# Self-attention and cross-attention of a decoder layer on one core: the batch loops written out, and VectorE's work in self-attention in another order

## The chip, the core and the metric

The kernel runs on one core of a Trainium2 chip. A core has five engines that run side by side, each from its own queue and in its order: TensorE (PE in the profile; its weight loads are listed apart as PEld), VectorE (DVE), ScalarE (ACT), GpSimd (POOL) and SyncE (SP), which here only issues transfers. They wait for each other by semaphores. The metric is the time of one execution in microseconds (us) on the device; lower is better.

## The reference

The layer takes x (16 batches, 100 tokens, 512 features) and a context (16 batches, 722 keys, 512 features). In short:

```python
x = x + attn(layernorm(x))            # 64 heads of 32 in four branches, rotary positions, sinks
x = x + xattn(layernorm(x), ctx)      # 16 heads of 32, softmax over the 32 largest of 722 scores
x = x + ffn(layernorm(x))             # a product with a 512x512 matrix in the frequency domain
```

```python
# attn, per batch (B, H, T, DH)
q = rope(rms_norm(X @ WQ + bQ));  k = rope(X @ WK + bK);  v = X @ WV + bV
w = (q @ k.T) / |k| * branch_mask
probs = softmax([w, tanh(sink)])
out = probs[..., :T] @ v + probs[..., T:] * v_nulls
y = mean over the four branches of (out @ WO + bO)
```

What the change touches is in `attn`: rms_norm and rope of the projected q and k, and the softmax's denominator.

## The kernel before

The program has three parts, one after the other. `self_program` computes the first line of the reference for all batches and writes x1 to DRAM. `spectral_program` (not touched) builds the 512x512 matrix M of the last line. `cross_program` computes the second and third line.

**Self-attention.** One batch's q of three branches and its k are 2048 columns, four segments of 512. The function `body(b, ...)` of each engine is written as a software pipeline: a body does the attention of batch b (`cur`), the output of batch b-1 (`prev`), the projections of batch b+1 (`nxt`) and the layer norm of batch b+2 (`far`). `each_batch` writes out bodies -2 to 1 and 14 to 16 and puts a hardware loop (`eng.Fori`) around one body for batches 2 to 13. Inside the loop the wait counts are computed in registers from the loop's counter.

TensorE's body, in order: it spreads the reciprocal of the denominators over partitions (L629), turns segment 0 of the rotated q and k (`turn(0)`, four transposes, L616), computes the values of the third branch (`value(2)`, L600), `turn(1)`, transposes the next batch's normalised x (L642), `turn(2)`, `turn(3)`, the output product of the batch before (L651), and then four times a group of four heads' scores and one segment of the next batch's projection (both L88 to L90, each product split in three), two value products (also L88 to L90), the denominators (L708) and the numerators (L716).

VectorE's body: `low(g)` (L506) makes the low half of the turned segment g, after ScalarE has made its high half; `turn(1)` waits for `low(0)` and `turn(3)` for `low(1)`, since they write into the same PSUM bank. Three products by the spread reciprocals (L530) and two sums (L532, L535) give the context, for which the output product waits. `biased(n)` (L511) takes segment n of the projection out of PSUM; `squares(n)` (L517, L520) sums ScalarE's squares of it; GpSimd raises these sums to the power -0.5 (`power(n)`, L362); `rope(n)` (seven instructions, L483 to L491) scales and rotates the segment. `statistics` (L95 to L97) and `normalised` (L501) are the layer norm of batch b+2. The reciprocal of the denominators (L579) waits for L708 of TensorE, and L629 of the next body waits for it. GpSimd also masks the scores of each group of four heads (L351) ahead of `power(1)`.

The second value product on TensorE waits until `biased(3)` has emptied its PSUM bank.

**Cross-attention.** It works on 13 tiles of scores a batch (128 rows of 722 keys), in seven steps of two tiles. VectorE finds the 32 largest of each row by four rounds of MAX8 and MATCH_REPLACE8 (L1368 to L1390), and also does a few layer norm instructions (L1400 is one). ScalarE does the exponentials and copies, GpSimd subtractions and low halves. `each_batch` there loops seven times over two bodies, batches 1 to 14, and writes out the others.

Of the kernel before, what the change touches and what calls it, by code (L numbers as in the profile page):

```python
# [23 lines left out]
B, T, D, KV = 16, 100, 512, 722  # L24
# [155 lines left out]
def self_program(nc, A, x1_dram, y3_dram):  # L180
# [5 lines left out]
    QC = NQK // 128  # L186
# [4 lines left out]
    with ExitStack() as ctx:  # L191
# [90 lines left out]
        def each_batch(eng, body):  # L282


            body(At(-2), cur=False, prev=False, nxt=False, far=True)
            body(At(-1), cur=False, prev=False, nxt=True, far=True)
            body(At(0), cur=True, prev=False, nxt=True, far=True)
            body(At(1), cur=True, prev=True, nxt=True, far=True)
            with eng.Fori(2, B - 2) as i:
                body(At(0, i), cur=True, prev=True, nxt=True, far=True)  # L290
            body(At(B - 2), cur=True, prev=True, nxt=True, far=False)
            body(At(B - 1), cur=True, prev=True, nxt=False, far=False)
            body(At(B), cur=False, prev=True, nxt=False, far=False)
# [151 lines left out]
        def _(dve):  # L445
# [29 lines left out]
            def body(b, cur, prev, nxt, far):  # L475
# [49 lines left out]
                if prev:  # L525

                    dve.wait_ge(num_mm, b.count(HK, 0))
                    for n in range(NL):
                        dve.wait_ge(rb_ready, b.count(NL, n + 1 - NL))
                        dve.tensor_tensor(rb[:, n, :], pq[:, n, 0:CC * T], rb[:, n, :], ALU.mult).then_inc(num_used, 1)  # L530
                    dve.wait_ge(num_used, b.count(NL, 2 - NL))
                    order.mark(dve.tensor_tensor(rb[:, 0, :], rb[:, 0, :], rb[:, 1, :], ALU.add))  # L532
                    dve.wait_ge(num_used, b.count(NL, 0))
                    order.after(order.n)
                    dve.tensor_tensor(rb[:, 0, :], rb[:, 0, :], rb[:, 2, :], ALU.add).then_inc(ctx_ready, 1)  # L535
                if cur:
                    for g in range(1, QC // 4):
                        low(g)
                if nxt:

                    dve.wait_ge(xT_hi, bn.count(1, 1))
# [12 lines left out]
                if nxt:  # L554
                    at = bn.const if bn.reg is None else bn.reg + bn.const
                    dve.tensor_reduce(xsum[:, :, bass.ds(at, 1)], xT[:, :, :], AX.X, ALU.add).then_inc(sum_ready, 1)

                    biased(0)
                    biased(1)
                    squares(0)  # L560
                    biased(2)
                    squares(1)
                    rope(0)
                    biased(3)
                    squares(2)
                    squares(3)
                if far:
                    statistics()
                if cur and not nxt:

                    each = lambda t: t[:, :].unsqueeze(2).broadcast_to((128, CC, B))
# [6 lines left out]
                    dve.wait_ge(den_mm, b.count(HK, HK))  # L578
                    dve.reciprocal(rden[:, :], pq[:, 3, 0:T]).then_inc(rden_ready, 1)  # L579
                if nxt:  # L580
                    rope(1)
                    rope(2)
                if far:
                    normalised()
                if nxt:
                    rope(3)
                order.finish()
            each_batch(dve, body)

# [162 lines left out]
def cross_program(nc, A, M, x1_dram, y3_dram, out_dram):  # L752
# [17 lines left out]
    with ExitStack() as ctx:  # L770
# [91 lines left out]
        def each_batch(eng, body):  # L862

            body(At(-1), 1, tiles=False, prev=False, nxt=True)
            body(At(0), 0, tiles=True, prev=False, nxt=True)
            with eng.Fori(0, (B - 2) // 2) as i:
                body(At(1, i, 2), 1, tiles=True, prev=True, nxt=True)
                body(At(2, i, 2), 0, tiles=True, prev=True, nxt=True)
            body(At(B - 1), 1, tiles=True, prev=True, nxt=False)
            body(At(B), 0, tiles=False, prev=True, nxt=False)  # L870

# [619 lines left out]
```

## Time and profile before

| | |
|---|---|
| three runs | 2444.17, 2447.41, 2450.51 us; median 2447.41 |
| the profiled execution | 2448.53 us, of which its span is 2446.7 |
| self-attention, first to last score group (batch 0 to batch 15) | 78.76 to 716.33 us of the span |
| cross-attention, from VectorE's first steady stretch | about 900 to 2446 us of the span |
| busy over the span | TensorE 87%, VectorE 81%, ScalarE 52%, GpSimd 53% |

The busy shares are means over two parts with different limits: in self-attention VectorE is busy for 64% of the time and TensorE for 90%, in cross-attention VectorE for 98%. So the two are read apart. A bracket in a row of the timeline gives the time that the engine was idle ahead of the instruction and what ended it; "issue" is idle time in which the engine waited for nothing that the profile shows.

### The profile page before, as it was taken

The numbers are of one execution on the slowest core, as the hardware profiler recorded it, in microseconds if no ns is written. First come the engines' busy times: TensorE is split into PE (matmuls) and PEld (weight loads), VectorE is DVE, ScalarE is ACT, GpSimd is POOL, SyncE is SP. The second block draws the span as 40 slices with busy tenths as digits, with TensorE's granted clock in tenths as the row PEclk, the third lists the DMA queues.
The fourth block names the chain that finished last, engine by engine and source line by source line (L and its number), as shares of the span: only waits on it lengthen the run. The fifth ranks groups of instructions, "written<-read, shape, count | busy, mean of one in ns | idle before, by whom it ended". The sixth has DMA issues, their size and how long they took to land. (4 is left out here: it accounts for less than half of the span.)

```text
span 2446.7 us, 54297 instructions
## 1 busy us (share of the span) xinstructions
PE 2122.6 (87%) x19760; PEld 1650.1 (67%) x19760; DVE 1977.5 (81%) x3663; ACT 1265.8 (52%) x2464; POOL 1285.2 (53%) x1473
## 2 busy tenths in 40 slices
PE   2898999989897378999999999999899899899966
PEld 1565555656563267877778778778778788788754
DVE  4666565666642149999999999999999999999995
ACT  3232323223221147666666666676676676676652
POOL 2564554636450336566456565565565565555542
PEclk9999998989888689999999999999999999999987
DMA  5000000000002610010001000100100010001000
GB/s 180 11 15 17 13 17 13 10 19 11 14 15 91 161 28 18 13 36 18 20 25 29 21 24 13 37 18 19 37 18 19 25 29 19 25 13 36 5 5 11
DMA packets 41485, 70.11 MB, mean 29 GB/s; under 512 B 4638, under 2 KB 21166, under 8 KB 41260
## 3 DMA queue, kind: packets, MB, share of 16 engines
q1 hardware_dynamic: 35868, 56.31, 7.6%
q0 software_dynamic: 3632, 7.58, 1.3%
q10 hardware_dynamic: 1760, 3.28, 0.5%
q8 instruction: 134, 2.20, 0.4%
q14 instruction: 91, 0.75, 0.1%
HBM read 60.54 MB, written 9.86 MB: 29 GB/s over the span
## 5 line engine op out<-in xcount | busy, mean ns | idle before, releaser
L1390 DVE MATCH_REPLACE8 ca_W<-ca_top,ca_W 128x722 f32<-128x722 f32 (+1 forms) x624 | 553.0, 892 | 0.0
L1378 DVE MAX8 ca_top<-ca_W 128x8 f32<-128x722 f32 (+1 forms) x624 | 536.7, 897 | 2.2
L997 POOL TENSOR_TENSOR ca_S<-ca_S,ca_W 128x722 f32<-128x722 f32 (+1 forms) x208 | 358.6, 1743 | 276.0 <-ACT ca_W L1253 276.0
L1368 DVE MAX8 ca_top<-ca_S 128x8 f32<-128x722 f32 (+1 forms) x208 | 179.0, 898 | 64.9 <-ACT ca_S L1270 49.3
L1275 ACT ACTIVATE ca_PT<-ca_pT 128x768 f32<-128x768 f32 (+1 forms) x208 | 163.6, 786 | 129.4 <-PE ca_pT L1128 129.4
L974 POOL TENSOR_TENSOR ca_KL<-ca_K,ca_KH 128x384 fp32r<-128x384 f32 (+1 forms) x128 | 122.6, 958 | 183.3 <-ACT ca_KH L1245 180.5
L1253 ACT ACTIVATE ca_W<-ca_W,ca_shift 128x722 f32<-128x722 f32 (+1 forms) x208 | 186.0, 894 | 61.8 <-DVE ca_W L1390 61.4
L1161 PE MATMUL ca_pO<-ca_PT,ca_V 128*32 128x56 f32 (+5 forms) x4608 | 217.0, 225 | 0.0
L88 PE MATMUL ca_pS<-ca_KH,ca_QH 128*128 128x362 f32 (+1 forms) x384 | 150.7, 393 | 70.7 <-ACT ca_S L1270 63.5
L1263 ACT ACTIVATE ca_S<-ca_S,ca_shift 128x722 f32<-128x722 f32 (+1 forms) x208 | 175.8, 891 | 65.3 <-POOL ca_shift L989 65.2
L362 POOL TENSOR_TENSOR sa_ss<-sa_ss,sa_minus_half 100x16 f32<-100x16 f32 x64 | 192.3, 3023 | 22.1 <-DVE sa_ss L520 22.1
L88 PE MATMUL ca_pF<-ca_cH,ca_WkH 128*128 128x338 f32 (+1 forms) x512 | 190.5, 372 | 8.2 <-POOL ca_cL L982 4.7
L1128 PE MATMUL ca_pT<-ca_ident,ca_S 128*128 128x128 f32 (+1 forms) x1248 | 179.1, 280 | 19.3 <-issue 19.3
L1270 ACT ACTIVATE ca_S<-ca_pS 128x722 f32<-128x722 f32 (+1 forms) x208 | 159.3, 766 | 56.8 <-PE ca_pS L90 52.4
L1161 PEld LDWEIGHTS ca_pO<-ca_PT,ca_V 128*32 128x32 f32 x4608 | 186.3, 111 | 0.0
L1387 DVE MATCH_REPLACE8 ca_W<-ca_top,ca_S 128x722 f32<-128x722 f32 (+1 forms) x208 | 184.4, 892 | 0.0
L89 PE MATMUL ca_pF<-ca_cL,ca_WkH 128*128 128x338 f32 (+1 forms) x512 | 176.7, 345 | 0.0
L90 PE MATMUL ca_pF<-ca_cH,ca_WkL 128*128 128x338 f32 (+1 forms) x512 | 175.9, 344 | 0.0
L435 ACT ACTIVATE sa_E<-sa_pq 100x300 f32<-100x300 f32 x256 | 86.2, 426 | 169.5 <-PE sa_pq L90 169.5
L1128 PEld LDWEIGHTS ca_pT<-ca_ident,ca_S 128*128 128x128 f32 (+1 forms) x1248 | 132.8, 142 | 44.4 <-issue 29.7
L344 POOL TENSOR_TENSOR sa_step<-sa_minus_half 1x1 f32<-1x1 f32 x64 | 14.2, 222 | 282.5 <-ACT sa_E L435 282.5
L351 POOL TENSOR_SCALAR_AFFINE_SELECT sa_E<-sa_E 100x400 f32<-100x400 f32 x256 | 150.0, 586 | 17.8
(213 smaller groups left out, 5286.2 us busy)
## 6 DMA issues: line engine op xcount, KB each, us to landing
ca_raw<-in_ctxT SPq DMA_DIRECT2D x32, 384.0 KB, 4.0
ca_raw<-in_ctxT SPq DMA_DIRECT2D x32, 338.0 KB, 3.0
sa_xin<-in_x SPq DMA_DIRECT2D x16, 200.0 KB
sa_xres<-in_x SPq DMA_DIRECT2D x16, 200.0 KB
x_scratch<-sa_x SPq DMA_DIRECT2D x16, 200.0 KB
x_scratch<-y_scratch POOLq DMA_DIRECT2D x16, 200.0 KB, 13.7
ca_xin<-x_scratch SPq DMA_DIRECT2D x16, 200.0 KB
ca_x<-x_scratch SPq DMA_DIRECT2D x16, 200.0 KB
```

The source lines that it names most:

```text
L88: pe.matmul(out, ah, bh, start=start, stop=False)
L89: pe.matmul(out, ah, bl, start=False, stop=False)
L90: return pe.matmul(out, al, bh, start=False, stop=stop)
L362: pool.tensor_tensor(part, part, minus_half[:, 0:NH], ALU.pow).then_inc(norm_ready, 1)
L997: pool.tensor_tensor(S[k][rows, :], S[k][rows, :], W[r][rows, :], ALU.subtract).then_inc(p_ready, 1)
L1128: last = pe.transpose(pT[:, 128 * k:128 * k + t.rows], S[slot(t)][0:t.rows, KEY0[k]:KEY0[k] + 128], ident[0:t.rows, 0:t.rows])
L1161: last = pe.matmul(pO[to:to + DH, NUM + at + q.start:NUM + at + q.stop], V[tp][:, k, 128 * g + to:128 * g + to + DH], PT[:, k, cols], star ...
L1253: act.activation(W[r][rows, :], W[r][rows, :], ACT.Exp, bias=shift[rows, r:r + 1], scale=SCALE).then_inc(f_ready, 1)
L1368: dve.max(top[r][rows, 0:8], S[slot(t)][rows, :]).then_inc(peaked, 1)
L1378: n_of[t.i] = order.mark(dve.max(top[r][rows, 8 * k:8 * k + 8], W[r][rows, :]))
L1387: dve.match_replace(W[r][rows, :], eight, S[slot(t)][rows, :], REMOVED).then_inc(removed, 1)
L1390: ins = dve.match_replace(W[r][rows, :], eight, W[r][rows, :], REMOVED)
```

## The change

1. In `self_program` the loop over batches 2 to 13 is written out: twelve bodies in a row on each engine. In `cross_program` the loop over pairs of batches is written out too: fourteen bodies. No register is needed any more for the wait counts and the addresses of transfers, and no branch is taken.
2. VectorE's body in self-attention has another order. `rope(0)` stands behind `biased(3)`, `squares(2)` and `squares(3)`; `rope(1)` stands behind `statistics`, ahead of the reciprocal; `normalised` stands behind `rope(3)`; and `low(1)` stands ahead of the two sums of the context. No instruction is added or removed, and no other engine's order changes.

```diff
-            with eng.Fori(2, B - 2) as i:
-                body(At(0, i), cur=True, prev=True, nxt=True, far=True)
+            for n in range(2, B - 2):
+                body(At(n), cur=True, prev=True, nxt=True, far=True)
...
                         dve.tensor_tensor(rb[:, n, :], pq[:, n, 0:CC * T], rb[:, n, :], ALU.mult).then_inc(num_used, 1)
+                if cur:
+                    low(1)
+                if prev:
                     dve.wait_ge(num_used, b.count(NL, 2 - NL))
                     order.mark(dve.tensor_tensor(rb[:, 0, :], rb[:, 0, :], rb[:, 1, :], ALU.add))
...
                 if cur:
-                    for g in range(1, QC // 4):
-                        low(g)
+                    low(2)
+                    low(3)
...
                     squares(0)
                     biased(2)
                     squares(1)
-                    rope(0)
                     biased(3)
                     squares(2)
                     squares(3)
+                    rope(0)
                 if far:
                     statistics()
+                if nxt:
+                    rope(1)
...
                     dve.reciprocal(rden[:, :], pq[:, 3, 0:T]).then_inc(rden_ready, 1)
                 if nxt:
-                    rope(1)
                     rope(2)
+                    rope(3)
                 if far:
                     normalised()
-                if nxt:
-                    rope(3)
...
-            with eng.Fori(0, (B - 2) // 2) as i:
-                body(At(1, i, 2), 1, tiles=True, prev=True, nxt=True)
-                body(At(2, i, 2), 0, tiles=True, prev=True, nxt=True)
+            for n in range(1, B - 1):
+                body(At(n), n % 2, tiles=True, prev=True, nxt=True)
```

VectorE in a body of self-attention, from the layer norm's statistics to the first instruction of the second rotated segment. Before:

```order
L95 BN_STATS sa_stats<-sa_xin 100x6
L96 BN_AGGR sa_mv<-sa_stats 100x2
L97 TENSOR_SCALAR sa_mv<-sa_mv 100x1
L579 RECIPROCAL sa_rden<-sa_pq 128x100
L483 TENSOR_TENSOR sa_qk<-sa_qk,sa_ss 100x512
```

The same place now:

```order
L97 TENSOR_SCALAR sa_mv<-sa_mv 100x1
L483 TENSOR_TENSOR sa_qk<-sa_qk,sa_ss 100x512
L484 TENSOR_TENSOR sa_tmp<-sa_qk,sa_sin 100x256
L485 TENSOR_TENSOR sa_rq<-sa_qk,sa_cos 100x16x16
L486 TENSOR_TENSOR sa_tmp<-sa_qk,sa_cos 100x256
L487 TENSOR_TENSOR sa_rq<-sa_qk,sa_sin 100x16x16
L489 TENSOR_TENSOR sa_rq<-sa_rq,sa_tmp 100x16x16
L491 TENSOR_TENSOR sa_rq<-sa_rq,sa_tmp 100x16x16
L584 RECIPROCAL sa_rden<-sa_pq 128x100
```

One whole rotation, seven instructions, stands between the statistics and the reciprocal, where nothing stood. (L584 is the line of the reciprocal in the changed kernel.)

VectorE from the end of one body of self-attention to the start of the next. Before, at the loop's end:

```order
L491 TENSOR_TENSOR sa_rq<-sa_rq,sa_tmp 100x16x16
L82 ISA
L289 REGISTER_ALU
L289 COMPARE_AND_BRANCH
L506 TENSOR_TENSOR sa_qkTl<-sa_pp,sa_qkTh 128x400
L530 TENSOR_TENSOR sa_rb<-sa_pq,sa_rb 128x400 x3
L532 TENSOR_TENSOR sa_rb<-sa_rb 128x400
L535 TENSOR_TENSOR sa_rb<-sa_rb 128x400
```

The same place now:

```order
L82 ISA
L506 TENSOR_TENSOR sa_qkTl<-sa_pp,sa_qkTh 128x400
L530 TENSOR_TENSOR sa_rb<-sa_pq,sa_rb 128x400 x3
L506 TENSOR_TENSOR sa_qkTl<-sa_pp,sa_qkTh 128x400
L535 TENSOR_TENSOR sa_rb<-sa_rb 128x400
L538 TENSOR_TENSOR sa_rb<-sa_rb 128x400
```

The branch is gone, and the second L506 has moved ahead of the two sums (L535 and L538 now).

VectorE between the last tile of an even batch and the first tiles of the next in cross-attention, before:

```order
L1390 MATCH_REPLACE ca_W0<-ca_top0,ca_W0 64x722
L82 ISA
L866 REGISTER_ALU
L866 COMPARE_AND_BRANCH
L1368 MAX ca_top2<-ca_S0 128x8
```

Written out, the two instructions of L866 are not there, on this and on the four other engines.

## Rows read from the trace of the kernel before

**Rows 1.** Windows: length, busy us of each engine (instructions), granted clock, DMA share, GB/s.

```profile
163.70:675.20 511.50, 462.38 (x5329) 297.69 (x5328) 325.41 (x684) 155.16 (x372) 273.31 (x300) 0.92 0.05 14
```

**Rows 2.** Timeline (start, duration, line, [idle before]): first scores, batches 0 and 15.

```profile
78.76 0.60 PE L88 MATMUL sa_pq<-sa_qkTh 32*100 32x300 f32 x4 [1.20 <-DVE sa_qkTl L506]
...
716.33 0.41 PE L88 MATMUL sa_pq<-sa_qkTh 32*100 32x300 f32 x4
```

**Rows 3.** TensorE's waits in 163.7 to 675.2 us: total, times, longest.

```profile
PE sa_pp L616 <- DVE sa_qkTl L506: 44.5, 24, 2.3
PE sa_pp L88 <- DVE sa_qk L511: 4.6, 12, 0.4
```

**Rows 4.** Timeline of TensorE around one loop pass.

```profile
410.44 0.79 PE L616 MATMUL sa_pp<-sa_ident,sa_rq 100*128 100x100 f32 x4 [2.31 <-DVE sa_qkTl L506]
...
414.21 5.18 PE L651 MATMUL sa_pw<-sa_WO,sa_rb 128*100 128x512 f32 x8
419.33 0.41 PE L88 MATMUL sa_pq<-sa_qkTh 32*100 32x300 f32 x4
...
433.27 0.39 PE L90 MATMUL sa_pp<-sa_WqkH,sa_xTl 128*100 128x512 f32 x1
...
441.86 2.24 PE L716 MATMUL sa_pq<-sa_E,sa_V 101*32 101x100 f32 x96
```

**Rows 5.** Timeline of VectorE in the same pass and the start of the next.

```profile
436.09 0.68 DVE L511 TENSOR_TENSOR sa_qk<-sa_pp,sa_bias_qk 100x512 f32<-100x512 f32 x1
...
438.07 0.68 DVE L95 BATCH_NORM_STATS2 sa_stats<-sa_xin 100x6 f32<-100x512 f32 x1
...
439.00 0.15 DVE L97 TENSOR_SCALAR sa_mv<-sa_mv 100x1 f32<-100x1 f32 x1
442.19 0.78 DVE L579 RECIPROCAL sa_rden<-sa_pq 128x100 f32<-128x100 f32 x1 [3.03 <-PE sa_pq L708]
442.89 0.63 DVE L483 TENSOR_TENSOR sa_qk<-sa_qk,sa_ss 100x512 f32<-100x512 f32 x1
...
445.57 0.68 DVE L483 TENSOR_TENSOR sa_qk<-sa_qk,sa_ss 100x512 f32<-100x512 f32 x1
...
448.31 0.54 DVE L501 TENSOR_SCALAR sa_xn<-sa_xin,sa_mv,sa_rstd 100x512 f32<-100x512 f32 x1
...
451.81 0.57 DVE L506 TENSOR_TENSOR sa_qkTl<-sa_pp,sa_qkTh 128x400 fp32r<-128x400 f32 x1 [0.23 <-issue]
...
454.41 0.57 DVE L535 TENSOR_TENSOR sa_rb<-sa_rb 128x400 f32<-128x400 f32 x1
```

**Rows 6.** The first rotation's start, and GpSimd's mask (L351) and powers (L362).

```profile
431.76 0.68 DVE L483 TENSOR_TENSOR sa_qk<-sa_qk,sa_ss 100x512 f32<-100x512 f32 x1
...
434.59 2.58 POOL L351 TENSOR_SCALAR_AFFINE_SELECT sa_E<-sa_E 100x400 f32<-100x400 f32 x4
437.14 9.13 POOL L362 TENSOR_TENSOR sa_ss<-sa_ss,sa_minus_half 100x16 f32<-100x16 f32 x3
```

**Rows 7.** Windows around the wait of rows 4, columns as in rows 1.

```profile
407.10:410.50 3.40, 1.09 (x4) 0.26 (x3) 3.14 (x9) 0.60 (x1) 0.00 (x0) 1.00 0.35 120
410.60:417.30 6.70, 5.74 (x20) 3.54 (x20) 4.78 (x10) 2.01 (x4) 0.00 (x0) 0.50 0.00 0
```

**Rows 8.** VectorE's waits from 907.2 to 2336.5 us; windows of two single batches.

```profile
DVE ca_top L1368 <- issue: 15.1, 6, 3.5
...
998.99:1093.13 94.14, 88.42 (x786) 74.50 (x784) 93.51 (x168) 63.72 (x120) 55.84 (x65) 0.98 0.08 24
...
1190.56:1286.54 95.98, 90.08 (x844) 75.79 (x842) 95.34 (x169) 67.80 (x131) 59.84 (x68) 1.00 0.09 24
```

**Rows 9.** TensorE's instruction queue, 60 to 190 us; a written-out batch; cross-attention's loop ends.

```profile
q8 instruction: 10, 0.16, 0.5%
...
699.99 0.71 PE L716 MATMUL sa_pq<-sa_E,sa_V 101*32 101x100 f32 x19 [0.36 <-issue]
...
PE ca_pT L1128 <- issue: 19.3, 6, 4.3
```

## The prediction

> **What bounds the kernel now.** I read the windows first, since the busy shares of the whole span mix two parts. In self-attention TensorE works 462 of 511.5 us and VectorE 325 [rows 1]; in cross-attention VectorE works 93.5 of the 94.1 us of a batch [rows 8]. The change has to be priced in each by itself.
>
> Self-attention takes 637.6 us from the first scores of batch 0 to those of batch 15, fifteen passes of 42.5 us [rows 2], and the twelve passes of the loop take 511.5 / 12 = 42.6 us [rows 1]. TensorE's waits name what ends last there: 24 waits, two a pass, for L506 of VectorE, 44.5 us or 3.7 us a pass, and one a pass of 0.38 us for `biased(3)`, L511 [rows 3]. The timeline shows the long one: `turn(1)` waits 2.31 us for `low(0)` [rows 4], and `low(0)` is the first thing in VectorE's body, so what holds it is what stands at the end of the body before. There VectorE first sat idle for 3.03 us ahead of the reciprocal, which waits for the denominators, and had three rotations still to do behind it [rows 5]. The idle 3 us and the 2.3 us that TensorE waits 10 us later are the same time, lost once on each engine.
>
> The wait costs twice. In the window of the wait TensorE works 1.09 of 3.4 us, and in the 6.7 us behind it the granted clock is 0.50, that is 1.2 instead of 2.4 GHz [rows 7]. The output product falls into it and takes 5.18 us for eight matmuls [rows 4].
>
> Cross-attention runs at VectorE's pace. Its only named idle time between 907 and 2336 us is 15.1 us of "issue" in 6 places [rows 8]: the six taken branches of the loop over pairs of batches. TensorE shows the same six, 19.3 us [rows 9].
>
> **The order in self-attention.** I follow the new chain from TensorE's last projection matmul of a pass to the next scores. Up to there nothing changes: scores at 419.33, last projection matmul over at 433.66, 14.3 us [rows 4]. Then, by the starts of rows 5:
> - `biased(3)`, `squares(2)`, `squares(3)`: 436.09 to 438.07, 2.0 us. They start at 433.7 now, not at 436.09, because `rope(0)` no longer stands ahead. TensorE's 0.38 us wait goes with it.
> - `rope(0)`: 4.33 us today (431.76 to 436.09, rows 5 and 6), because GpSimd masks beside it; a rotation beside GpSimd's powers takes 2.68 us (442.89 to 445.57). Now it starts at 435.7, when the last mask has some 1.0 to 1.4 us left [rows 6]. I take 3.1, between 2.7 and 4.3, near the first because most of the mask is past.
> - `statistics`: 438.07 to 439.15, 1.1 us.
> - `rope(1)`: 2.7 us. It needs `power(1)`, a third of 9.13 us behind the mask, so at 440.2 today and rather earlier when the mask is less disturbed [rows 6]. VectorE arrives at 433.7 + 2.0 + 3.1 + 1.1 = 439.9. The two meet, at a cost of 0 to 0.3 us.
> - reciprocal 0.7 us (442.19 to 442.89). It starts at 442.6 instead of 442.19, while TensorE, 0.38 us earlier, is done with the numerators at 443.7 [rows 4, 5]. The spread of the reciprocals, which alone waits for it, needs it at 443.4 or so: it is just in time, and each later 0.1 us would be paid.
> - `rope(2)` and `rope(3)`: 2.7 us each, `normalised` 0.5, and no branch ahead of `low(0)` (0.23 us of issue today).
> - `low(0)`, three products and the two sums: 451.81 to 454.98, 3.2 us, and `low(1)` between them, 0.5.
>
> Sum: 2.0 + 3.1 + 1.1 + 2.7 + 0.7 + 5.4 + 0.5 + 3.2 + 0.5 = 19.2 us. So `low(0)` ends some 2 us earlier against TensorE, and the 2.31 us wait shrinks to 0.3. What is late next: `turn(3)` waits for `low(1)` still, about 0.7 us, and the output product, which waited for nothing, now waits 0.6 us for the second sum, because TensorE has caught up. `low(1)` ahead of the sums serves the first and delays the second by 0.5. Then the output product: eight matmuls of 0.43 at the full clock, 3.5 us (half of the 5.18 us were run at the low clock). A pass is 14.3 + 19.2 + 3.5 = 37.0 us, with 0.3 us for the semaphores between, 37.3.
>
> **The clock.** This decides 2.6 us of it: 1.7 in the output product and 0.9 in the transposes around it. Today TensorE works 32% of the window that comes ahead of the low clock [rows 7]. In the new chain the 3.4 us from `value(2)` to the output product hold 1.6 us of waits, so it works about half. I take it that the clock mostly stays up and put 0.5 us a pass on the passes where it does not.
>
> **The loops.** In 190 to 655 us no instruction is loaded at all, the loop's bodies stay resident; ahead of it, in 60 to 190 us, TensorE's queue loads 10 blocks of 16 KB for about three batches [rows 9]. Written out, every batch pays that. The load itself is 0.5% of the DMA engines. The price is where TensorE runs out of instructions in the short matmuls of L708, L716 and L629: the one that the profile names, in a batch written out behind the loop, is 0.36 us [rows 9]. I take 0.4 us a pass; bounds 0, since VectorE's chain may hide it, and 0.7 for two of them.
>
> The Trainium skill (Runtime: NRT & Kernel Launch, "Instruction fetch mechanics") says that a straight stream of instructions is loaded ahead and costs next to nothing, and that only a branch out of the loaded window stalls. By it this term would be 0 and the time 6 us less. The trace bears out the branch (up to 3.5 us of issue at a loop end of cross-attention) but shows a stall in a straight stream too, so I keep the row's price.
>
> A pass is 37.3 + 0.5 + 0.4 = 38.2 us. Against 42.5 that is 4.3, and for fifteen passes 64.5 us, all on the path, since the next scores wait for it.
>
> **Cross-attention.** Removed: 15.1 us of issue, at full price, since VectorE has no other wait there for it to fall into. A second gain is likelier than not. The batch ahead of the loop's first branch takes 94.14 us, one behind a branch that holds none takes 95.98, with 1.8 us more of VectorE's work and the same instruction count [rows 8]: after the stall its instructions meet GpSimd's at other moments. Six batches could give up to 1.8 us each back, or all could settle in the worse phase. Bounds -3 and +11; I take 4. No stall for code is added: these bodies were loaded anew in every pass already. Sum 19 us.
>
> **Total.** From the profiled execution, 2448.5 us (1.1 above the median of the three runs, which I ignore): 2448.5 - 64.5 - 19 = 2365.
>
> **Rivals.**
> 1. The clock still falls in every pass. For it: half of the time idle is not much, and several short waits remain. Then a pass is 37.3 + 2.6 + 0.4 = 40.3 us, the gain 2.2 x 15 = 33, with 19 from cross-attention 2396.
> 2. GpSimd sets the pace: `rope(0)` keeps its 4.33 us beside the mask, 1.2 more, and everything behind it on VectorE comes later, the reciprocal too, at 443.8. That is 18 us for fifteen passes, and TensorE's idle time grows by as much, so the clock falls oftener: 2383 to 2414. Against it: the mask ends at 437.1 today even with the rotation beside it. The Trainium skill (SBUF — State Buffer, "SBUF: two separate sides") makes this stronger: a VectorE instruction with two SBUF inputs and a GpSimd one lock each other out for a whole instruction. Beside the masks the trace agrees; beside the powers, which are two-input instructions of 3 us, it does not (rotations at 2.68 us), so I move no rotation's price for them.
> 3. The move gives nothing, because the 3.03 us of idle time only change place: `power(1)` late, the reciprocal behind it. Left are the loops, 19 us, and 0.3 us a pass for the branch: 2425.
> 4. Slower: the code of TensorE does not come in time. In L708 and L716 it takes 192 matmuls and as many weight loads in 4.3 us, so a block of 256 instructions lasts 2.9 us there. If each of about four blocks a pass cost what a loop end in cross-attention costs, 19.3 / 6 = 3.2 us [rows 9], twelve passes would lose 154 us: 2519. It turns to slower from 83.5 / 48 = 1.7 us a block. The 0.36 us stall of a batch that is written out already speaks against it.
>
> **How the numbers follow.** Forecast 0.58, rival 1 0.17, rival 2 0.12, rival 3 0.09, rival 4 0.04. The range: down to 2343, with no term for code or clock (fifteen passes at 37.3, 78 us) and 11 from the phases in cross-attention (26 us); up to 2400, which takes in rival 1 and the better half of rival 2. Outside lie rivals 3 and 4 and a little more. 0.3% of this time is 7 us, about what a measurement of this kernel can tell from no change; faster holds for all rivals but the last and a remnant: faster 0.95, same 0.01, slower 0.04.
>
> **What would show it.** Right: the first scores of batches 0 and 15 stand 573 us apart (560 to 605); VectorE's idle time ahead of the reciprocal is gone; TensorE's wait for `low(0)` is under 0.6 us; the output product takes 3.5 us and the granted clock of self-attention is over 0.95; no "issue" row on VectorE in cross-attention, and batches of 94 to 95 us. Wrong: an output product still at 5 us (rival 1), a first rotation at 4 us (2), TensorE waiting for the reciprocal ahead of L629 (2, 3), gaps of "issue" over 1 us in L708 to L716 of every batch (4).

## The result and the profile after

The changed kernel takes 2351.4 us (median of four runs, 2346.9 to 2352.0) against 2448.7 us before (four runs, 2444.2 to 2450.5): a ratio of 0.960, 95% interval 0.958 to 0.962. The forecast was 2365, with a range of 2343 to 2400. The profiled execution has a span of 2349.5 us, 97.2 less than the 2446.7 of before. I split that by the places that the prediction had named.

| stretch | before, us | after, us | gain | forecast |
|---|---|---|---|---|
| first scores of batch 0 to those of batch 15 (self-attention, 15 passes) | 637.6 | 565.7 | 71.9 | 64.5 |
| from there to the third tile of cross-attention's batch 0 | 190.9 | 188.9 | 2.0 | 0 |
| third tile of batch 0 to that of batch 15 (cross-attention) | 1429.3 | 1411.6 | 17.7 | 19 |
| from there to the end | 110.2 | 104.5 | 5.7 | 0 |

The first place to look at is the timeline of TensorE at the first scores of batches 0 and 15, the lines that answer to [rows 2]:

```profile
78.83 0.60 PE L88 MATMUL sa_pq<-sa_qkTh 32*100 32x300 f32 x4 [1.20 <-DVE sa_qkTl L506]
...
644.52 0.41 PE L88 MATMUL sa_pq<-sa_qkTh 32*100 32x300 f32 x4
```

They stand 565.7 us apart, 37.7 us a pass. Next, the windows of after (columns as in [rows 1]): most of self-attention, one pass of the usual length, and one of two that are longer.

```profile
163.70:630.00 466.30, 448.91 (x5529) 296.71 (x5531) 318.50 (x706) 158.89 (x383) 280.35 (x317) 0.99 0.06 18
...
231.85:269.05 37.20, 35.64 (x445) 23.61 (x444) 25.72 (x57) 12.89 (x31) 22.12 (x25) 1.00 0.06 18
269.05:307.96 38.91, 37.41 (x445) 24.14 (x444) 25.70 (x57) 12.87 (x31) 22.12 (x25) 0.96 0.06 18
```

TensorE now works 448.9 of 466.3 us, 96%, where it worked 462.4 of 511.5, 90% [rows 1]; the mean granted clock went from 0.92 to 0.99. The two passes have the same instructions and the same work on the other engines. They differ in the clock alone, 1.00 against 0.96, and by 1.7 us.

TensorE's waits between 150 and 620 us (total, times, longest) answer to [rows 3]:

```profile
PE sa_pp L619 <- DVE sa_qkTl L506: 9.7, 20, 0.8
PE sa_pw L654 <- DVE sa_rb L538: 8.0, 13, 0.6
PE sa_pt L632 <- issue: 0.2, 1, 0.2
```

The waits for `low`, 44.5 us in the twelve passes of [rows 3], are 9.7 us in this stretch of some twelve and a half, the 4.6 us for `biased(3)` are gone, and a new wait stands in their place, that of the output product for the second sum. The timeline of TensorE at the end of the usual pass shows where each lies (compare [rows 4]):

```profile
262.40 0.53 PE L619 MATMUL sa_pp<-sa_ident,sa_rq 100*128 100x100 f32 x4 [0.17 <-DVE sa_qkTl L506]
...
264.32 0.54 PE L619 MATMUL sa_pp<-sa_ident,sa_rq 100*128 100x100 f32 x4 [0.70 <-DVE sa_qkTl L506]
265.48 3.65 PE L654 MATMUL sa_pw<-sa_WO,sa_rb 128*100 128x512 f32 x8 [0.62 <-DVE sa_rb L538]
269.06 0.41 PE L88 MATMUL sa_pq<-sa_qkTh 32*100 32x300 f32 x4
```

`turn(1)` waits 0.17 us instead of 2.31, `turn(3)` 0.70, the output product 0.62, and that product takes 3.65 us instead of 5.18. VectorE in the same pass, the lines for [rows 5]:

```profile
246.20 0.69 DVE L511 TENSOR_TENSOR sa_qk<-sa_pp,sa_bias_qk 100x512 f32<-100x512 f32 x1 [1.84 <-PE sa_pp L90]
...
248.21 0.68 DVE L483 TENSOR_TENSOR sa_qk<-sa_qk,sa_ss 100x512 f32<-100x512 f32 x1
...
251.19 0.68 DVE L95 BATCH_NORM_STATS2 sa_stats<-sa_xin 100x6 f32<-100x512 f32 x1
...
252.36 0.70 DVE L483 TENSOR_TENSOR sa_qk<-sa_qk,sa_ss 100x512 f32<-100x512 f32 x1
...
255.12 0.78 DVE L584 RECIPROCAL sa_rden<-sa_pq 128x100 f32<-128x100 f32 x1
255.81 0.63 DVE L483 TENSOR_TENSOR sa_qk<-sa_qk,sa_ss 100x512 f32<-100x512 f32 x1
...
258.49 0.68 DVE L483 TENSOR_TENSOR sa_qk<-sa_qk,sa_ss 100x512 f32<-100x512 f32 x1
...
261.68 0.57 DVE L506 TENSOR_TENSOR sa_qkTl<-sa_pp,sa_qkTh 128x400 fp32r<-128x400 f32 x1
...
264.76 0.57 DVE L538 TENSOR_TENSOR sa_rb<-sa_rb 128x400 f32<-128x400 f32 x1
```

No idle time is left behind `biased(3)`: the reciprocal follows the second rotation at once. `rope(0)` takes 2.98 us (248.21 to 251.19) where it took 4.33. GpSimd, for [rows 6], shows why, and also what is near behind:

```profile
246.39 2.90 POOL L351 TENSOR_SCALAR_AFFINE_SELECT sa_E<-sa_E 100x400 f32<-100x400 f32 x4
249.26 8.80 POOL L362 TENSOR_TENSOR sa_ss<-sa_ss,sa_minus_half 100x16 f32<-100x16 f32 x3
```

The last mask is over at 249.3, about a third of the way through `rope(0)`. The three powers end near 252.2, 255.1 and 258.06; the rotations that need them begin at 252.36, 255.81 and 258.49, so none is late, by 0.2 to 0.7 us.

Instruction loading, for [rows 9]: between 190 and 600 us TensorE's queue (q8) now brings code in all the time. The only trace of it in TensorE's rows is the single 0.2 us of "issue" above, at 482.58 us. It falls into the eleventh pass, which takes 37.4 us at a clock of 1.00, where the usual pass takes 37.2.

```profile
q8 instruction: 38, 0.62, 0.6%
q14 instruction: 12, 0.10, 0.1%
```

In cross-attention VectorE's waits from 907 to 2250 us hold one "issue" row of 0.3 us where [rows 8] had 15.1 us in six places:

```profile
DVE ca_top L1380 <- issue: 0.3, 1, 0.3
```

Its batches take 93.6 to 95.1 us, but for the first and the last (91.8 and 92.1).

The end was not in the forecast. Windows over the last 54 us of before and the last 48 us of after, with the same work on VectorE (25.00 us in both):

```profile
2393.00:2446.70 53.70, 33.66 (x279) 20.68 (x277) 25.00 (x45) 14.28 (x29) 15.48 (x18) 0.73 0.04 12
```

```profile
2301.50:2349.50 48.00, 28.70 (x280) 18.31 (x278) 25.00 (x45) 14.32 (x29) 15.45 (x18) 0.86 0.05 13
```

TensorE is busy 5 us less with one matmul more, at a granted clock of 0.86 instead of 0.73. The three waits of VectorE there, for one line of ScalarE (L1289 before, L1291 now) and for two products, went from 9.7 + 7.7 + 6.8 to 8.5 + 6.6 + 3.8 us.

### The profile page after: what moved, and what is told of

Read it like the earlier page. It is cut to its first block and busy times, and to the rows that moved or that the text cites. A ratio compares the mean times of both kernels' runs of the same rounds, so it can differ in the third digit from the quotient of the medians.

```text
span 2349.5 us, 50955 instructions
## 1 busy us (share of the span) xinstructions
PE 2076.7 (88%) x19760; PEld 1630.2 (69%) x19760; DVE 1954.6 (83%) x3663; ACT 1266.2 (54%) x2464; POOL 1276.8 (54%) x1473
## 5 line engine op out<-in xcount | busy, mean ns | idle before, releaser
L362 POOL TENSOR_TENSOR sa_ss<-sa_ss,sa_minus_half 100x16 f32<-100x16 f32 x64 | 187.1, 2941 | 20.0 <-DVE sa_ss L520 20.0
L511 DVE TENSOR_TENSOR sa_qk<-sa_pp,sa_bias_qk 100x512 f32<-100x512 f32 x64 | 44.2, 691 | 147.8 <-PE sa_pp L90 147.8
L984 POOL TENSOR_TENSOR ca_cL<-ca_raw,ca_cH 128x768 fp32r<-128x768 f32 (+1 forms) x64 | 111.7, 1766 | 85.6 <-ACT ca_cH L1232 85.6
L351 POOL TENSOR_SCALAR_AFFINE_SELECT sa_E<-sa_E 100x400 f32<-100x400 f32 x256 | 146.6, 573 | 17.8
```

Of the source, the lines that this page charges most:

```text
L362: pool.tensor_tensor(part, part, minus_half[:, 0:NH], ALU.pow).then_inc(norm_ready, 1)
```

## The experiments

**The order alone, and the loops alone.** These split the change in two. In `order_only` both loops stand and VectorE has the new order:

```diff
-            for n in range(2, B - 2):
-                body(At(n), cur=True, prev=True, nxt=True, far=True)
+            with eng.Fori(2, B - 2) as i:
+                body(At(0, i), cur=True, prev=True, nxt=True, far=True)
...
-            for n in range(1, B - 1):
-                body(At(n), n % 2, tiles=True, prev=True, nxt=True)
+            with eng.Fori(0, (B - 2) // 2) as i:
+                body(At(1, i, 2), 1, tiles=True, prev=True, nxt=True)
+                body(At(2, i, 2), 0, tiles=True, prev=True, nxt=True)
```

> VectorE's new order with both loops kept. Theory A (the parts add up; the order makes the self-attention gain by itself): the passes go from 42.5 to 37.3 + 0.3 for the branch on VectorE = 37.6 us, 74 us less, and cross-attention stays: 2375 us, ratio 0.970. Rival B (the order only pays when the branch and the register instructions are gone as well): passes of 39 to 41 us, 2396 to 2426 us.

Measured: 2373.8 us, ratio 0.970 (0.968 to 0.972). The scores of batches 0 and 15 stand 565.0 us apart, as in the changed kernel (565.7). So in self-attention the order gives everything; writing the loop out neither costs nor gives anything there. Its passes are 37.2 us (three of them 38.8 to 38.9, the first 39.5), those of the written-out program 37.2 as well (two of 38.9, the first 41.4). In cross-attention VectorE still has its six gaps:

```profile
DVE ca_top L1371 <- issue: 17.1, 6, 3.5
```

`loops_only` is the kernel before with the two loops written out as in the change (the reverse of the diff above, applied to before).

> Both loops written out, VectorE's old order. Theory A: cross-attention gives its 17.7 us (six gaps of 15.1 us and some of the slower VectorE instructions behind them), and each of twelve passes of self-attention 0.3 us for the branch, and 1 us where the low clock lasts 3.4 instead of 6.8 us as in the two batches that were written out already: 2448.7 - 18 - 4 to -16 = 2415 to 2427 us, ratio 0.986 to 0.991. Rival B: if the order needs the loops gone and the loops the order, less than 18 us: over 2431. Rival C (loading code costs TensorE 0.4 us or more a pass): cross-attention's gain is partly eaten, 2427 to 2436.

Measured: 2413.7 us, ratio 0.987 (0.984 to 0.989), just under the 2415 to 2427 that I had expected. Cross-attention is that of the changed kernel, batch by batch within 0.1 us. Self-attention takes 629.4 us instead of 637.6. TensorE's waits between 163.7 and 675.2 us are nearly those of before (43.6 us for `low`, 24 times), but the granted clock of that stretch is 0.95 instead of 0.92:

```profile
163.70:675.20 511.50, 462.91 (x5394) 297.39 (x5394) 327.73 (x690) 159.10 (x385) 278.05 (x311) 0.95 0.05 16
```

The two parts by themselves give 74 and 34 us beside the same runs of before, 108 together, the whole 97. Most of the overlap is these 8 us of self-attention: with the old order the written-out program has no branch ahead of `low(0)` (0.23 us a pass), and the clock still falls in every pass, but stays low for 3.4 us instead of 6.9 in ten of the fifteen (0.96 and 0.92 over a pass); with the new order the loop costs nothing there any more. Most of the rest is in the end of the kernel, which is 4.0 us shorter in the trace of `order_only`, 5.7 in that of `loops_only` and 5.7 with both.

**One loop alone.** `cross_loop` keeps the loop in cross-attention's program only (the second half of the diff above).

> The changed kernel with the loop of cross-attention kept. Theory A: it lacks the 17.7 us of cross-attention and nothing else: 2351.4 + 17.7 = 2369 us, six VectorE gaps of issue of 15 us in all, and batches of 95 to 96 us behind a loop end. Rival D (the gaps alone are the cost, the slower VectorE instructions behind them have another cause): 2366.5, and batches without a loop end of 94.2.

Measured: 2388.4 us, ratio 0.976 (0.973 to 0.978). I had forecast 2369, and it is 15 us slower even than `order_only`, which has both loops. VectorE's waits from 907 to 2290 us:

```profile
DVE ca_top L1371 <- issue: 25.2, 5, 5.3
DVE ca_top L1371 <- ACT ca_top L1259: 5.8, 1, 5.8
```

The second row is the sixth loop end, which the profile puts down to ScalarE; its place and length are the same as the others'. So the six gaps are 31.0 us and not 17.1, and 13.9 of the 15 us are there. The loop's body is word for word the same; the program ahead of it is longer. The trace also holds the branch and register instructions of VectorE's queue, which the timeline leaves out. In `order_only` there is one pause at each of the six loop ends, 3.0 to 3.9 us behind the branch; in `cross_loop` there are two, 2.7 to 3.3 us behind the branch and 2.3 to 3.1 us more one instruction later. My guess was that the place of the loop in its blocks of code (the pieces in which instructions are loaded) decides whether the branch stalls VectorE once or twice. A first try of it put sixteen no-operations on VectorE ahead of the loop:

> The kernel cross_loop (the changed one with the loop of cross-attention kept) with 16 empty instructions on VectorE ahead of that loop, once. Theory I (in cross_loop VectorE stalls twice at a loop end, 2.7 us and 2.9 us one instruction later, because the loop's first instruction is the last of its block of code and the next block has to be loaded as well; where the code ahead of it has another length, one load is enough): VectorE's gaps go from 5.2 to 2.3 to 3.5 us each and the time from 2388 to 2366 to 2374 us. Rival J (the longer gaps come from the time at which the loads meet other transfers or from the other engines): gaps and time as cross_loop, 2385 to 2391 us.

Measured: 2387.2 us, ratio 0.975 (0.973 to 0.977), gaps as in `cross_loop` (32.0 us in six, two pauses at each). That settled nothing: the trace has no row for a no-operation, and I can't say that they took up any place. So I put instructions there that the trace does show:

```diff
+            for _ in range(16):
+                order.after(order.mark(dve.memset(stats[:, :], 0.0)))
             each_batch(dve, body)
```

> cross_loop (the new kernel with the loop kept in the cross-attention's program) with sixteen small memsets added on VectorE ahead of that loop, so that all of its instructions behind them lie sixteen places further on. They cost about 2 us once. cross_loop took 2388 us, with VectorE idle 4.9 to 5.8 us at every loop end; order_only, with the same loop body behind a shorter program, idled 2.3 to 3.5 us there. Theory I (the place of the loop in its code blocks decides whether the branch stalls VectorE once or twice): sixteen places move the target, the gaps fall to 2.3 to 3.5 us, and the time to about 2372 to 2377 us. Theory J (the double stall comes from something else, such as the length of the written-out program ahead): gaps stay at 4.9 to 5.8 us and the time at 2387 to 2391 us. If the gaps lie between or become longer still, the place matters, but by another rule than one block.

Measured: 2369.7 us, ratio 0.970 (0.968 to 0.971), 19 us faster with sixteen instructions more (15 us when each kernel is taken against its own runs of before; in the traces 17.9 us of cross-attention, batch 0 to batch 15). The first loop end that I compared, in the timeline of VectorE, first of `cross_loop` and then of `cross_loop_padded`:

```profile
1291.12 0.89 DVE L1393 MATCH_REPLACE8 ca_W<-ca_top,ca_W 64x722 f32<-64x722 f32 x1
1297.14 1.73 DVE L1371 MAX8 ca_top<-ca_S 128x8 f32<-128x722 f32 x2 [5.14 <-issue]
```

```profile
1287.46 0.89 DVE L1393 MATCH_REPLACE8 ca_W<-ca_top,ca_W 64x722 f32<-64x722 f32 x1
1290.65 1.73 DVE L1371 MAX8 ca_top<-ca_S 128x8 f32<-128x722 f32 x2 [2.31 <-issue]
```

and over all of cross-attention in `cross_loop_padded`:

```profile
DVE ca_top L1371 <- issue: 13.9, 6, 2.6
```

The second pause is gone at all six loop ends: the queue's instructions show one, 2.7 to 3.1 us behind the branch. So what stands ahead of the loop decides whether the branch stalls VectorE once or twice, and the place of the body is the likely reason. What exactly has to fall where (I think of the branch's target and the end of a block of code) was not measured, and one shift was tried. The length of a single pause is not set by the place alone: `filled` (next) has VectorE's program of before word for word and idles 18.7 us at the same six loop ends, where before has 15.1.

**The clock by itself.** `filled` is the kernel before with eight matmuls on TensorE ahead of `turn(1)`, into a bank that is free there and whose result nobody reads. They lie in its long wait and change no other engine's work.

```diff
                     value(2)
+                    if prev:
+                        pe.wait_ge(rb_ready, b.count(NL, 0))
+                        for _ in range(8):
+                            pe.matmul(pw[0:T, :], xTh[:, 0, :], WvH[:, 0, piece(0)], start=True, stop=True)
                     turn(1)
```

> The kernel before, with eight matmuls of 512 columns that nobody reads written into a free PSUM bank by TensorE ahead of turn(1), in place of 1.8 of its 2.3 us wait. No wait is removed. Theory A (the low clock is a price of its own beside the wait, 2.2 to 2.6 us of the 5.2 us a pass, and comes from the wait): the granted clock of self-attention goes over 0.95, the output product takes 3.5 to 4 us, passes of 40.0 to 40.5 us: 2411 to 2416 us, ratio 0.985 to 0.987. Rival E (the clock does not depend on that wait, or its low stretch hides beside VectorE's chain): passes stay at 42.5 or grow by the fill, 2447 to 2455 us.

Measured: 2422.6 us, ratio 0.990 (0.987 to 0.992). I had expected 2411 to 2416, with every pass near 40.2 us. More work on the busiest engine of self-attention still makes the kernel 1% faster. A window and TensorE's first row of waits, of `filled`, from 163.7 to 640 us:

```profile
163.70:640.00 476.30, 446.13 (x5364) 294.18 (x5362) 313.20 (x657) 149.19 (x362) 272.45 (x299) 0.98 0.05 15
```

```profile
PE sa_pp L616 <- DVE sa_qkTl L506: 25.6, 22, 1.9
```

The clock is 0.98, passes are alternately 40.2 and 41.7 us instead of 42.5 (the clock falls in the second of each pair), and 25.6 us of waits are left in the stretch. So the clock was a price of its own, 2.3 us in a pass in which it stays up, and some 22 us could be had without touching VectorE; the rest is the chain.

**The parts of the order.** `rope1_behind` is the changed kernel with the second rotation behind the reciprocal again.

```diff
                 if far:
                     statistics()
-                if nxt:
-                    rope(1)
...
                 if nxt:
+                    rope(1)
                     rope(2)
                     rope(3)
```

> The changed kernel with rope(1) behind the reciprocal again, the rest as changed. Theory A (this rotation in the idle time ahead of the reciprocal is the largest part of the order's gain): low(0) comes 1.5 to 2 us later, turn(1) waits that much, and the low clock comes back in most passes: passes of 39.0 to 41.0 us, 2378 to 2408 us. Rival G (the other moves alone remove the wait): passes under 38 us, under 2363 us.

Measured: 2394.5 us, ratio 0.978 (0.976 to 0.980), 43 us slower than the changed kernel. Passes take 38.9 to 42.0 us but for the first, and TensorE's waits from 163.7 to 640 us are

```profile
PE sa_pp L618 <- DVE sa_qkTl L506: 26.2, 22, 2.0
```

This one move carries the larger part of the gain, some 42 of the 72 us in self-attention (its first scores of batches 0 and 15 stand 607.6 us apart): 2.7 us of a rotation put into the idle time ahead of the reciprocal, and what of the clock goes with it.

`rope0_early` puts the first rotation ahead of `biased(3)` again.

```diff
                     squares(1)
+                    rope(0)
                     biased(3)
                     squares(2)
                     squares(3)
-                    rope(0)
```

> The changed kernel with rope(0) ahead of biased(3) again, the rest as changed. Theory A (the move counts because the rotation runs beside GpSimd's masks there, 4.3 instead of 2.9 us, and holds biased(3)): the second value product waits 0.38 us again, rope(1) starts at the end of power(1) instead of ahead of it, the reciprocal comes some 0.8 us later against the scores: passes of 37.9 to 38.3 us, 2361 to 2368 us, more if the clock falls oftener. Rival F (the idle 1.8 us of VectorE ahead of biased(3), which the changed order leaves open, is worth as much as the slower rotation costs): passes of 37.2 to 37.5, 2351 to 2355 us.

Measured: 2348.3 us, ratio 0.960 (0.958 to 0.962), the same as the changed kernel. VectorE's and TensorE's waits from 150 to 620 us hold one row each that is new and over 0.5 us in total:

```profile
DVE sa_qk L483 <- POOL sa_ss L362: 11.0, 12, 0.9
```

```profile
PE sa_pp L88 <- DVE sa_qk L511: 4.6, 12, 0.4
```

The rotation takes 4.3 us again (243.74 to 248.07 in one pass), beside GpSimd's masks. But then VectorE comes to `rope(1)` 0.9 us ahead of its power. Had it been earlier, it would have waited longer. A usual pass is 37.45 us instead of 37.2, which is 3.5 us in fourteen. Against it, the clock falls in none of the later passes, where it falls in two of the changed kernel (3.4 us), and the first pass takes 39.4 us instead of 41.4. The two kernels can't be told apart in time; that the clock falls less often because of this order is not shown by one trace of each. All that can be put down to this part of the change is 0.25 us in a usual pass.

`low1_behind` puts `low(1)` behind both sums again.

```diff
-                if cur:
-                    low(1)
                 if prev:
                     dve.wait_ge(num_used, b.count(NL, 2 - NL))
...
                 if cur:
+                    low(1)
                     low(2)
```

> The changed kernel with low(1) behind the two sums of the context again. Theory A: turn(3) comes 1.0 us later and the sums 0.5 us earlier, so that the output product waits for turn(3) instead of the second sum and starts 0.5 us later: passes of 37.7 us, 2359 us (2355 to 2364). Rival H (which of the two comes first does not matter, since the output product waits for both): 2351 +- 3 us.

Measured: 2358.2 us, ratio 0.963 (0.961 to 0.966). Its usual pass takes 37.53 us instead of 37.2, since `turn(3)` waits longer for `low(1)` and the output product behind it comes later, though its sum is there: TensorE's waits for `low` between 150 and 620 us are 23.1 us instead of 9.7, and that for the sum is gone. The place is worth 0.3 us a pass, 5 us in fifteen. The total can't tell as much: the medians are 7 us apart, but the intervals overlap, and in the traces other things move too. Self-attention as a whole is only 0.9 us longer (the clock falls in one later pass here instead of two, and the first is 1.5 us shorter). The end of the kernel is 6.4 us longer, where VectorE waits 25.2 us instead of 18.9.

**What is late next.** VectorE still idles 1.84 us ahead of `biased(3)`, while `statistics` (1.17 us) stands on the path. `stats_in_gap` moves it there:

```diff
                     squares(1)
+                    if far:
+                        statistics()
                     biased(3)
...
-                if far:
+                if far and not nxt:
                     statistics()
```

> The new kernel with the statistics of the input (1.17 us on VectorE) moved from between rope(0) and rope(1) to between squares(1) and biased(3), where VectorE idles 1.84 us. Theory K (VectorE alone sets the end of the pass): 1.1 us less in each of fifteen passes, 16 us, about 2335 us. Theory L (GpSimd is the next bound: it is busy without a pause from the third mask to its last power at 258.06, and rope(3) begins at 258.49): the second rotation waits for its power to 252.2 instead of 252.36, and the fourth can begin no more than 0.4 us earlier; passes shorter by 0.1 to 0.3 us, 2346 to 2350 us.

Measured: 2349.3 us, ratio 0.961 (0.960 to 0.963). Nothing is gained. VectorE's row of waits from 150 to 620 us that the changed kernel does not have:

```profile
DVE sa_qk L483 <- POOL sa_ss L362: 14.0, 12, 1.2
```

The 1.17 us that were moved away are now 1.2 us of waiting for GpSimd's second power. In `stats_power` GpSimd does that power ahead of its fourth mask:

```diff
                 if cur:
                     mask(2)
+                if nxt:
+                    power(1)
+                if cur:
                     mask(3)
                 if nxt:
-                    for n in range(1, QB):
+                    for n in range(2, QB):
```

> As stats_in_gap, with GpSimd's power of the second segment also put ahead of the fourth mask. The second rotation then never waits (its power is there at 249.2), but the fourth mask ends at 252.2 instead of 249.3, and TensorE's denominators, which began at 251.65, begin 0.6 us later. GpSimd's last power ends at 258.0 as before. Theory L (GpSimd's sum of work is the bound): rope(3) from 258.1 instead of 258.49, passes shorter by 0.3 to 0.4 us, about 2345 us. Theory K: 2335 us. Theory M (TensorE's wait for the mask reaches the output): passes longer by 0.2 to 0.6 us, 2354 to 2360 us.

Measured: 2350.7 us, ratio 0.962 (0.960 to 0.963), where I had expected 2345; passes of 37.4 to 37.9 us behind the first. Now TensorE waits for the mask, and the output product for the sum as before:

```profile
PE sa_pw L659 <- DVE sa_rb L541: 7.9, 13, 0.6
PE sa_pq L716 <- POOL sa_E L351: 6.5, 12, 0.5
DVE sa_qkTl L509 <- ACT sa_qkTh L428: 2.7, 8, 0.6
```

The first rotation lies beside the mask again and takes 4.1 us (248.01 to 252.12), which eats the 1.17 us. The third row is VectorE's, in the same stretch: `low(1)` now comes before ScalarE has made its high half. GpSimd works without a pause from the third mask to the last power, and whichever of its pieces comes later is waited for. The last experiment also puts the first sum ahead of `low(1)`, on top of `stats_power`:

```diff
+                if prev:
+                    dve.wait_ge(num_used, b.count(NL, 2 - NL))
+                    order.mark(dve.tensor_tensor(rb[:, 0, :], rb[:, 0, :], rb[:, 1, :], ALU.add))
                 if cur:
                     low(1)
                 if prev:
-                    dve.wait_ge(num_used, b.count(NL, 2 - NL))
-                    order.mark(dve.tensor_tensor(rb[:, 0, :], rb[:, 0, :], rb[:, 1, :], ALU.add))
                     dve.wait_ge(num_used, b.count(NL, 0))
```

> As stats_power, with the first of the two sums of products put ahead of low(1) on VectorE, so that the pause between the two dependent sums (0.1 us) is covered by low(1), and the output product may begin earlier, while turn(3), which waits for low(1), begins 0.5 us later. Forecast: turn(3) still ends ahead of the second sum, passes 0.1 us shorter than in stats_power, about 2344 us. The rival: TensorE comes to the output product late behind turn(3), passes as long or 0.3 us longer, 2345 to 2350 us.

Measured: 2342.4 us (2340.5 to 2343.5), ratio 0.958 (0.957 to 0.960), 8 us less than `stats_power` beside the same runs of before, and the fastest kernel of this study. TensorE's rows of waits from 150 to 620 us, and the end of one pass in its timeline:

```profile
PE sa_pp L625 <- DVE sa_qkTl L509: 7.9, 13, 0.9
PE sa_pq L717 <- POOL sa_E L351: 6.5, 12, 0.5
```

```profile
263.21 0.53 PE L625 MATMUL sa_pp<-sa_ident,sa_rq 100*128 100x100 f32 x4 [0.74 <-DVE sa_qkTl L509]
263.69 3.65 PE L660 MATMUL sa_pw<-sa_WO,sa_rb 128*100 128x512 f32 x8
```

The output product no longer waits. On VectorE the two dependent sums stood 0.67 us apart, start to start, for 0.57 us of work (264.09 and 264.76 in the changed kernel); now `low(1)` lies between them, three instructions follow each other every 0.48 us in a usual pass, and the second sum is there when `turn(3)` is done. Passes are 36.98 to 37.25 us behind the first, 0.4 us shorter, where I had hoped for 0.1. In the pass shown the 0.4 us are made of two halves. The pause between the sums gives 0.19. The first sum stands where `low(1)` waited for ScalarE, and gives 0.2: in the same pass of `stats_power`, `low(1)` begins 1.65 us behind the first of the three products, and here the first sum begins 1.44 us behind it. In the changed kernel `low(1)` begins 1.44 us behind it too, so I would not expect this second half there. The sum's place alone, without the two other edits, was not tried. The interval of the ratio overlaps that of the changed kernel (0.958 to 0.962), which was timed beside other runs; the first scores of batches 0 and 15 stand 558.7 us apart here and 565.7 there.

## Why the prediction was right, and where it was not

**The chain of a pass.** Right, term by term. Forecast: 14.3 us from the scores to the last projection, then 19.2 on VectorE, 3.5 for the output product, 0.3 between, 37.3. Measured in the pass from 231.85: 14.35 us to `biased(3)` at 246.20, 19.13 from there to the end of the second sum (264.76 + 0.57 = 265.33), 0.15 to the output product, 3.58 to the next scores, 37.2. Inside the 19.13: `rope(0)` 2.98 (forecast 3.1, between the bounds of 2.7 and 4.3), the second power ready 0.2 us ahead of `rope(1)` (0 to 0.3 us late), the three waits 0.17, 0.70 and 0.62 us (0.3, 0.7 and 0.6). `rope1_behind` shows that the step was right for its reason: without the rotation in the idle time the largest wait for `low` is 2.0 us again and 43 us come back.

**The clock.** Right in size. The passes sum to 565.7 us, 7.7 more than fifteen of 37.2: 4.2 in the first one, 3.4 in two at 38.9, and 0.2 in the eleventh, the one with the "issue" row, less 0.2 in the last. That is 0.51 us a pass, forecast 0.5. Such close agreement is partly luck: in `order_only` the clock falls in three later passes and in `rope0_early` in none, and their first passes take 39.5 and 39.4 us. `filled` shows that the clock's price is apart from the chain's. What makes the clock fall in two of the later passes and not in the others is open. The two passes in the windows above have the same waits: in the second `turn(1)`, `turn(3)` and the output product wait 0.17, 0.70 and 0.63 us, and yet the product takes 5.34 us there and 3.65 in the first.

**The loading of code.** Wrong by nearly its whole size, 0.4 us a pass, 6 us. I had one row, a 0.36 us stall in one written-out batch [rows 9], and charged it to every pass. (I even charged it to fifteen, though three of them were written out before as well and had paid it already in the 42.5 us; twelve would have made it 4.8.) In the changed kernel TensorE's queue loads 38 blocks in 410 us, where `order_only` loads one in the same stretch, and the passes are 37.2 us in both. What is left is one "issue" row of 0.2 us and 0.2 us in one pass of fifteen. Most of the other kernels with written-out self-attention have such rows too, of up to 0.4 us behind the first pass and in no more than three passes; two of these passes in `cross_loop_padded` take 37.28 and 37.33 us, and in `low1_behind` a row of 0.39 us makes its pass no longer than the others. The kernels that keep this loop have no such row in the loop's passes. The statement of the Trainium skill (Runtime: NRT & Kernel Launch, "Instruction fetch mechanics") that a straight stream is loaded ahead would have given 0 here. That a straight stream can stall at all is shown by these rows, but the cost is next to nothing, and I should have given the trace's single row the weight of one row.

**Cross-attention.** Right: 17.7 us, forecast 19, of which 15.1 are the gaps and 2.6 the batches behind them, for which I took 4 out of -3 to 11. `loops_only` repeats it, and its gain does not depend on the order in self-attention. Why the batches give 2.6 us besides the gaps is not shown: I had put it down to the moments at which VectorE's instructions meet GpSimd's, and no run takes that apart. The experiments show, though, that the 15.1 us were a matter of luck. With another program ahead, the same six branches cost 31 us or 14.

**What I left out.** The end of the kernel, 5.7 us, and 2.0 us between the halves. The second is no more than the scatter of that stretch, which takes 185.3 to 191.4 us in the traces of the fourteen kernels, though the spectral program in it is the same in all. The changed kernel and six of the seven experiments in which cross-attention is written out have the same end, with 8.5, 3.8 and 6.6 us of waits for VectorE, 18.9 in all; `low1_behind` has 25.2. Those with a loop vary between 17.4 and 24.2 us. It goes with the granted clock: over the last 48 us that is 0.89 where the waits are 17.4 us (`filled`), 0.86 where they are 18.9, 0.70 in the kernel before and 0.66 in `low1_behind`. Why the clock in the last 50 us should depend on the loop ahead I can't show; no run was made for it.

The errors add up: 6.0 for code, 1.4 in the chain and clock, 7.7 left out, less 1.3 in cross-attention, are the 13.8 us, but for rounding, between forecast and measurement (83.5 and 97.2 us of gain).

**The rivals.** That the clock falls in every pass (2396): it falls in the first and in two others of fifteen. That GpSimd sets the pace with a first rotation of 4.3 us (2383 to 2414): not in the changed kernel, by 0.2 us. `rope0_early` has that rotation and loses 0.25 us a usual pass by it and not 1.2, since VectorE has 0.9 us to spare there before its next power. My price for this rival, 1.2 us a pass straight onto the path, was too high for that place; in `stats_power`, with the power there in time, the slower rotation is paid. That the move gives nothing (2425): refuted by `order_only`. That TensorE's code comes too late (2519): refuted by the passes of the changed kernel, whose longest wait for "issue" is 0.2 us.

## What to carry to other kernels

Idle time that an engine has ahead of a wait, followed by work that the other engine will need, can be lost twice, as here, and is worth filling with that work; but before moving the next piece, look at how far ahead of its use every other input stands (here 0.2 us for GpSimd's power), since that is all the next move could gain in `stats_in_gap`. If two dependent small instructions stand back to back, try an independent one between them (0.19 us a pass here). And when a loop with a hot body is kept, read its branch gaps after every edit of the code ahead of it.

## What I had not expected

- The same loop end costs VectorE 2.2 to 3.5 us or 4.7 to 6.1 us, with one pause or with two: 17.1, 31.0, 32.0 and 13.9 us in six places in four kernels with the same body that differ in what stands ahead of the loop. Sixteen small memsets ahead of the loop made the kernel 19 us faster.
- Eight superfluous matmuls in a wait made the kernel of before 1.0% faster, with the granted clock at 1.00 in every other pass: an output product of 3.60 us behind them instead of 5.18.
- Loading 38 blocks of code in 410 us beside a TensorE that is 96% busy cost no more than 0.2 us.
